# Cross attention's first half on one core: turning in two row tiles, key parts copied from SBUF to SBUF, and a new order of the work around them

## The reference

```
x = x + tanh(g_xattn) * xattn(ctx, ctx, layernorm(x), mask, wq, bq, wk, bk, wv, bv, wo, bo)
x = x + tanh(g_ffn)   * ffn(layernorm(x), Wq, Wk, Wv, Ws, Wd, Wo)

# xattn, for each batch
qh, kh, vh = heads(q @ wq + bq), heads(ctx @ wk + bk), heads(ctx @ wv + bv)
attn = softmax(qh @ kh.T / sqrt(16) + mask * -1e9)        # 16 x 112 x 375
out  = merge(attn @ vh) @ wo + bo
```

## Time and profile before

| what | value |
|---|---|
| median of 3 runs | 1317.49 us (1315.44 to 1321.64) |
| the profiled execution's own time | 1307.75 us |
| its span | 1306.0 us |
| mean granted TensorE clock | 0.986 of full speed |
| busy: PE, PEld, DVE, ACT, POOL | 1250.1, 1019.9, 860.6, 612.0, 549.9 us |
| first half, seen by its rows of PE | scores from 41 us to 660 us |

### The profile page before, as it was taken

How to read it: one execution, slowest core, us unless ns; L and a number is a source line. 1 busy time by engine, 2 the same in 40 slices (tenths; PEclk the granted TensorE clock), 3 DMA queues, 4 the chain that set the end, 5 groups by cost and what they waited for, 6 DMA issues and landing times. The chain is left out here.

```text
span 1306.0 us, 40359 instructions
## 1 busy us (share of the span) xinstructions
PE 1250.1 (96%) x15928; PEld 1019.9 (78%) x15928; DVE 860.6 (66%) x2455; ACT 612.0 (47%) x1353; POOL 549.9 (42%) x823
## 2 busy tenths in 40 slices
PE   5799999999999999999988999999999999999996
PEld 4577777777777777777767888888888888888885
DVE  2566766766776776766655676677667667766652
ACT  3455555556556556556423443443444344344431
POOL 3476676676676676666620221221222122122211
PEclk9899999999999999999989999999999999999997
DMA  8898897787787787786404665566566656656563
GB/s 231 186 192 189 192 202 166 165 185 162 164 185 159 159 185 155 159 189 145 104 18 110 145 138 156 139 141 143 138 143 138 157 136 141 142 139 148 138 156 91
DMA packets 262975, 200.21 MB, mean 153 GB/s; under 512 B 195906, under 2 KB 243844, under 8 KB 258692
## 3 DMA queue, kind: packets, MB, share of 16 engines
q1 hardware_dynamic: 262788, 197.64, 66.7%
HBM read 125.49 MB, written 72.11 MB: 151 GB/s over the span
## 5 line engine op out<-in xcount | busy, mean ns | idle before, releaser
L858 POOL TENSOR_SCALAR shifted<-raw,neg_max 112x375 f32<-112x375 f32 x512 | 304.5, 603 | 197.1 <-DVE neg_max L741 131.4
L741 DVE CUSTOM_DVE_ANT_0 raw<-bank_s,maskb 112x375 f32<-112x375 f32 x512 | 269.0, 544 | 119.4 <-issue 77.9
L653 ACT ACTIVATE probsT<-bank_t 128x448 f32<-128x448 f32 x384 | 181.1, 547 | 162.9 <-PE bank_t L446 162.9
L446 PE MATMUL bank_t<-ident,shifted 112*128 112x112 f32 x1536 | 170.7, 261 | 4.1 <-POOL shifted L858 4.1
L446 PEld LDWEIGHTS bank_t<-ident,shifted 112*128 112x128 f32 x1536 | 156.3, 141 | 22.7 <-POOL shifted L858 19.8
L437 PE MATMUL bank_s<-K_stack,Q_stack 128*112 128x375 bf16 x512 | 158.4, 337 | 12.8 <-DVE neg_max L741 8.2
L1381 DVE TENSOR_REDUCE max<-bank_s 112x4 f32<-112x448 f32 x128 | 78.7, 615 | 78.1 <-PE bank_s L1140 78.1
L1454 POOL TENSOR_TENSOR mix_bd<-pm_te,tok 128x448 f32<-128x448 f32 x32 | 30.4, 951 | 214.8 <-DMA pm_te<-pm_dram 214.8
L1092 PE MATMUL bank_ab<-xnT,wk2T 128*128 128x224 f32 x512 | 110.9, 360 | 0.6 <-ACT kT L1281 0.6
L1092 PE MATMUL bank_ab<-xnT,wq2T 128*128 128x224 f32 x512 | 110.8, 360 | 0.4 <-ACT qT L1273 0.4
L201 POOL TENSOR_SCALAR var_eps<-moments 112x1 f32<-112x1 f32 x32 | 7.1, 223 | 233.4 <-DVE moments L197 233.2
(11 more groups left out here) (141 smaller groups left out, 2227.4 us busy)
## 6 DMA issues: line engine op xcount, KB each, us to landing
K_stack<-k_dram SPq DMA_DIRECT2D x64, 562.5 KB, 7.3
k_dram<-k_parts SPq DMA_DIRECT2D x32, 562.5 KB, 5.0
att_dram<-att_q SPq DMA_DIRECT2D x32, 511.0 KB, 4.1
att_th<-att_dram SPq DMA_DIRECT2D x32, 511.0 KB, 4.3
v_dram<-mv SPq DMA_DIRECT2D x32, 455.0 KB, 6.1
v<-v_dram SPq DMA_DIRECT2D x32, 455.0 KB, 4.0
K_stack<-k_dram SPq DMA_DIRECT2D x32, 375.0 KB, 9.4
Q_stack<-q_dram SPq DMA_DIRECT2D x64, 168.0 KB, 9.3
```

Of the source, the lines that this page charges most:

```text
L446: last = nc.tensor.transpose(bank_t[0:KP, k, j * S:(j + 1) * S], shifted[:, g % 2, j, k * KP:(k + 1) * KP], c.ident[0:S, 0:S])
L653: act.activation(probsT[:, g % 2, k, :], bank_t[0:KP, k, 0:G * S], ACT.Exp).then_inc(exp_done, 1)
L741: dve.tensor_tensor_reduce(raw[:, g % 2, j, :], bank_s[h % 2][0:S, 0:S2], c.maskb[:, :], -1.0, -LEAST, ALU.add, ALU.min, neg_max[:, g % 2, ...
L858: pool.tensor_scalar(shifted[:, g % 2, j, 0:S2], raw[:, g % 2, j, :], -1.0, neg_max[:, g % 2, j:j + 1], ALU.mult, ALU.add).then_inc(shift_ ...
```

## The change

- **Turn.** Each transpose is cut into two: rows 0 to 63 and rows 64 to 111 of `shifted` (`HALVES`, as `switch` has it for its own turn). A unit u is one (chunk, head). The results lie in three banks as `PLACES` says, four stretches of 512, 480, 256 and 96 columns, and `exps` has one ACTIVATE for each. `turned` is raised once for a turn, not once for each bank, and PE waits for itself before unit 8 (`upper_done`).
- **Weigh.** `weigh(b, g)` stands ahead of `turn` of the next group wherever it can, and waits for all four exponentials.
- **Keys.** `k_dram` goes. SP copies each part from `k_parts` to its rows of `K_stack` with a transfer of its own for each half t: 128 partitions of 375 bf16 to 8 partitions of 16 x 375. That is 16 transfers for a batch, 6 ahead of the wait for the query parts and 10 behind the query stores. The wait for the scores of batch b-2 moves to the front.
- **Order.** On PE: S0 S1, weigh(b-1,2), transposes, turn(b-1,3), S2 S3 S4, keys 0, S5, weigh(b-1,3), turn(b,0), S6 S7, keys 1, heads_back, S8, weigh(b,0), turn(b,1), S9, heads_turn, S10, values 0 and 1, S11 S12, project, S13, turn_x, weigh(b,1), turn(b,2), S14 S15, values 2, queries. On DVE `split_queries` comes after the maxima of S0 to S3 instead of S0 and S1. On ACT `ctx_copy` comes ahead of `exps(b-1,3)`, and `copy_x` ahead of `exps(b,2)`.

```
+    DH = P // H
+    KEY_LOADS, QUERY_LOADS = 16 * EC * sum(n for _, n, _ in STACKED), 16 * len(STACKED)
+    UNITS, LOW = KC * G, z.S - 48
+    PLACES = ((0, 8, 0, 0, 0), (0, 10, 1, 1, 0), (8, 12, 0, 2, 0), (10, 12, 1, 2, 4 * LOW))
+    HALVES = ((0, LOW), (LOW, z.S))
...
             def exchange(b, p, i):
+                if not (isinstance(b, int) and b < 2):
+                    sp.wait_ge(scores_ready, H * (b - 1))
                 sp.wait_ge(k_split, b + 1)
-                sp.dma_start(by_partition(k_dram[bass.ds(b, 1)]), k_parts[:, p, :, :, :]).then_inc(k_stored[p], 16)
+                def stack_keys(blocks):
+                    for j, n, _ in blocks:
+                        for part in range(n):
+                            for t in range(EC):
+                                row = (j + part) * D + t * DH
+                                sp.dma_start(K_stack[row:row + DH, p, :, :],
+                                             k_parts[:, p, part, t, :]).then_inc(keys_stacked[p], 16)
+                stack_keys(STACKED[:1])
                 sp.wait_ge(q_split, b + 1)
...
-                if not (isinstance(b, int) and b < 2):
-                    sp.wait_ge(scores_ready, H * (b - 1))
-                sp.wait_ge(k_stored[p], 16 * i + 16)
-                for j, n, first in STACKED:
-                    sp.dma_start(K_stack[j * D:(j + n) * D, p, :, :].rearrange("d h k -> d (h k)"),
-                                 k_dram[bass.ds(b, 1), 0:n].rearrange("a q (d h) k -> (a q d) (h k)", h=H)).then_inc(stack_loaded[p], 16)
+                stack_keys(STACKED[1:])
                 sp.wait_ge(q_stored[p], 32 * i + 32)
...
...
             def turn(b, g, first):
                 pe.wait_ge(shift_done, H * b + G * g + G)
-                for k in range(KC):
-                    if not (first and g == 0):
-                        pe.wait_ge(exp_done, KC * (NG * b + g - 1) + k + 1)
-                    for j in range(G):
-                        last = nc.tensor.transpose(bank_t[0:KP, k, j * S:(j + 1) * S],
-                                                   shifted[:, g % 2, j, k * KP:(k + 1) * KP], c.ident[0:S, 0:S])
-                    last.then_inc(turned, 1)
+                if not (first and g == 0):
+                    pe.wait_ge(exp_done, len(PLACES) * (NG * b + g))
+                def one(half, u):
+                    lo, hi = HALVES[half]
+                    (bank, column), = [(bank, column + (u - first_u) * (hi - lo)) for first_u, end, h, bank, column in PLACES
+                                       if h == half and first_u <= u < end]
+                    k, j = u // G, u % G
+                    return nc.tensor.transpose(bank_t[0:KP, bank, column:column + hi - lo], shifted[lo:hi, g % 2, j, k * KP:(k + 1) * KP], c.ident[lo:hi, lo:hi])
+                for u in range(UNITS):
+                    if u == 8:
+                        pe.wait_ge(upper_done, NG * b + g + 1)
+                    one(0, u)
+                    last = one(1, (u + UNITS - 2) % UNITS)
+                    if u == 1:
+                        last.then_inc(upper_done, 1)
+                last.then_inc(turned, 1)
...
             def exps(b, g, first):
-                for k in range(KC):
-                    act.wait_ge(turned, KC * (NG * b + g) + k + 1)
-                    act.activation(probsT[:, g % 2, k, :], bank_t[0:KP, k, 0:G * S], ACT.Exp).then_inc(exp_done, 1)
+                act.wait_ge(turned, NG * b + g + 1)
+                for first_u, end, half, bank, column in PLACES:
+                    lo, hi = HALVES[half]
+                    act.activation(probsT[:, g % 2, first_u:end, lo:hi], bank_t[0:KP, bank, column:column + (end - first_u) * (hi - lo)].rearrange("p (u q) -> p u q", q=hi - lo),
+                                   ACT.Exp).then_inc(exp_done, 1)
```

More of the change, by code:

```diff
@@ L296, in cross @@
         k_rest_done, k_second, k_split = sem("k_rest_done"), sem("k_second"), sem("k_split")
-        k_stored = [sem(f"k_stored{i}") for i in range(2)]
-        stack_loaded = [sem(f"stack_loaded{i}") for i in range(2)]
+        keys_stacked = [sem(f"keys_stacked{i}") for i in range(2)]
+        queries_stacked = [sem(f"queries_stacked{i}") for i in range(2)]
         half_set = sem("half_set")
@@ L507, in body @@
                 if back:
-                    turn(b - 1, NG - 1, False)
-                S_(2)
+                    weigh(b - 1, 1 - p, NG - 2, False)
                 if ahead:
                     transposes(b + 2, i + 1, p)
-                S_(3)
                 if back:
-                    weigh(b - 1, 1 - p, NG - 1, False)
-                S_(4)
+                    turn(b - 1, NG - 1, False)
+                S_(2, 3, 4)
                 if ahead:
@@ L518, in body @@
                 S_(5)
+                if back:
+                    weigh(b - 1, 1 - p, NG - 1, False)
                 turn(b, 0, first)
@@ L530, in body @@
                 S_(8)
+                weigh(b, p, 0, first)
                 turn(b, 1, False)
@@ L540, in body @@
                     values(1 - p, 1).then_inc(va_ready, 1)
-                S_(11)
-                weigh(b, p, 1, False)
-                S_(12)
+                S_(11, 12)
                 if back:
@@ L552, in body @@
                     open_x(b + 2 - B)
+                weigh(b, p, 1, False)
+                turn(b, 2, False)
                 S_(14, 15)
@@ L600, in _ @@
             batches(pe, body)
+            weigh(B - 1, 1, NG - 2, False)
             turn(B - 1, NG - 1, False)
@@ L668, in body @@
                 second = isinstance(b, int) and b == 1
+                if ahead:
+                    ctx_copy(b + 2, p, False)
                 if not first:
@@ L671, in body @@
                 if ahead:
-                    ctx_copy(b + 2, p, False)
+                    key_copy(b + 2, p, i + 1, 0)
                 if not first:
                     heads_copy(b - 1, second)
-                if ahead:
-                    key_copy(b + 2, p, i + 1, 0)
                 exps(b, 0, first)
@@ L684, in body @@
                     key_second(b + 2, p)
+                if ahead:
+                    copy_x(b + 2)
                 exps(b, 2, False)
                 if ahead:
-                    copy_x(b + 2)
                     query_copy(b + 2, p, i + 1)
@@ L796, in body @@
                     o.moments_of(dve, c.X[0:S, b + 2 - B, :], b + 2 - B)
-                score_max(b, first, 0, 1)
+                score_max(b, first, *range(4))
                 if not first and not last:
                     split_queries(b + 1)
-                score_max(b, first, *range(2, 7))
+                score_max(b, first, *range(4, 7))
                 if ahead:
@@ L855, in shift @@
                     h = G * g + j
-                    free = [] if j or (first and g < 2) else [(turned, KC * (NG * b + g - 1))]
+                    free = [] if j or (first and g < 2) else [(turned, NG * b + g - 1)]
                     wait_all(pool, v_set, (scores_read, H * b + h + 1), *free)
```

19 lines of the change are left out of this document (8 added, 11 removed).

## The result

The changed kernel takes 1679.55 us (median of 4 runs, 1653.12 to 1687.08), the kernel before 1319.57 us beside it; the ratio is 1.2605 with a 95% interval of 1.2533 to 1.2677. It is formed from the undisturbed runs alone and so lies a little under the ratio of the medians. Forecast were 1308 us and a range up to 1480. The rival "keys late" had the sign, the place and, at its upper price of 1644 us, the size.

The account below looks back on a forecast made before the run. PE, busy 96%, was taken to bound the kernel at 19.41 us a batch; terms summed to 0.30 us saved a batch, 9 us over thirty, giving 1308 us, with an 8-in-10 range of 1288 to 1480 us.

Parts of the forecast that it names:

- keys late: Rival: S0 waits for `K_stack` or `Q_stack`; 1384 us at 1.13 us a transfer, 1644 at 1.76; chance 0.38.
- x: Time of one 96 KB key transfer from SBUF to 8 partitions; taken near the key store, SP's 0.47 us binding.
- the point where it turns: Time of one key transfer, 0.88 us, from which late stacks instead of PE's 19.1 us set the batch period.
- the signs that it named: Signs of being wrong: S0 waiting each batch, key transfers landing well over 2 us after issue, DMA share above 0.9.
- 10.3 + 10x: Time in us from a batch's S0 until the next stacks are ready, with ten key transfers ahead of the query loads.
- the late split: `split_queries` behind the maxima of S2 and S3: ends 5.65 us after S0 instead of 3.0; query stores issued until 6.6.
- SP's issue time: On SP's queue: 0.47 us for each key transfer, 7.5 us a batch for 16.
- The turn: On PE: 24 half transposes take 0.75 us instead of 1.15; four turns save 1.60 us a batch.
- S4 and S13: PE waits for score banks: S4 1.06 to 1.10 us behind S2, net cost 0.46; S13 1.47 behind S11, cost 0.29.
- PE's sum: PE's gain a batch: 1.60 - 0.45 - 0.46 - 0.29 - 0.10 = 0.30 us, 9 us over thirty batches.
- PE's own waits eat the gain: Rival: `upper_done` and dearer transpose pairs lose up to 0.46 us a batch, halfway 1320 us; chance 0.14.
- What was called hidden: On ACT: a fourth exponential, 0 to 0.43 us, and later exponentials, covered by weighting over 2.5 us behind its turn.

Follow-up runs that it names:

- the run with four fewer: Changed kernel without the last four of the ten key transfers behind the query stores from the third batch on: 1450.64 us, ratio 1.0996.

## Why the prediction was wrong, point by point

**The step that failed** is the choice of x, the time of one key transfer: "I take x near the key store, since pieces and source are its own, and consecutive transfers go to different partitions". The store's row told of the source and the pieces; what binds is the destination. Measured in the changed kernel: 1.75 us at the 55 GB/s of 431 to 436 us, 1.7 by the run with four fewer, against 0.47 taken and 0.88 as the point where it turns. That the form of the copy isn't to blame is shown by the run that changed the rows alone. The earlier trace rows had the warning, 215 GB/s into 48 or 32 partitions against 334 into 112, and the argument gave it less weight than the likeness of source. The prediction called this its weakest choice and gave late keys a chance of 0.38, but its range of 8 in 10 ended at x about 1.45. Of the signs that it named, S0 waited in every batch, but the DMA share wasn't above 0.9: it was 0.58 at the 55 GB/s.

The Trainium skill, page "SBUF — State Buffer", section "Door 1: The DMA port swizzle", put four neighbouring partitions on one port of 27 GB/s; its estimate was x = 1.76 us and 1640 us, measured were 1.7 to 1.75 and 1680. By that rule neighbouring rows reach 2 ports, rows 2 apart 4 and rows 4 apart 8, estimated 54, 109 and 218 GB/s; the traces have 55, 97 and 144, the last at SP's issue rate. The runs don't measure a port itself.

**What followed from x.** The rival's 10.3 + 10x with a late start of the last ten gave 30.3 us for the period at x = 1.76, measured 30.5. That is in part luck. The same sum gives 27.7 us with the early split (30.3 - 2.65), measured 23.4: x is no constant, it averages at most 1.46 us there. So the late split, which by that sum costs 2.65 us a batch or 80 us, is a large part of the loss where transfers are slow: with neighbouring rows an early one gives back 228 of the 360 us, with keys through DRAM 33. The sum also had the query stores issued from 5.65 us after S0; it was 427.67 - 420.30 = 7.4, with the clock at the lower level behind the wait.

**SP's issue time** was 0.65 us a transfer, not 0.47: the row used was for three loads of another shape. It does no harm in the changed kernel with rows 4 apart and three query loads. With four query loads and 12 key transfers behind the stores SP needs 2.6 us more, of the 3.3 by which the period is longer (22.9 against 19.6 us on average).

**The turn.** 411.10 - 410.21 = 0.89 us with one change of shape; the sum had 0.75 + 0.09 = 0.84. That is 0.2 us a batch of the 0.30 forecast.

**S4 and S13.** S4 starts 1.11 us behind S2 (forecast 1.06 to 1.10), S13 1.48 behind S11 (forecast 1.47).

**PE's sum.** Forecast 0.30 us a batch, 9 us. The kernel with keys through DRAM and early split, which is this sum without any wait for a stack, stands at 1.0022, with a period of 19.5 us where the sum had 19.1: nothing gained. The rival "PE's own waits eat the gain" is what this part came to; the dearer turn is half of it, the context's transposes waited 0.17 us for the query copies instead of 0.10, and the rest wasn't followed up.

**The late split** was costed only for the straight keys. With keys through DRAM it makes S0 wait 0.87 us and costs 2.4% (1.0266 against 1.0022). Nothing needed it late: with the split early again the new order runs at 19.5 us a batch.

**What was called hidden.** The fourth exponential is hidden. The later start of all four was said to be covered because each weighting comes well behind its turn; in the new order no such wait stands among those of the kernel with keys through DRAM and early split, and the turn alone in the old one shows the price without the cover and without the moved `copy_x`, 1.1%.

**Left open.** Why the batches of the kernel with the early split get 142 GB/s at one time and 55 at another, and with it why an early split gives back so much. That it has to do with which transfers are in flight together is shown by the two runs with another order; that they overlap across ways, or that the engines fall into step on one pair of ways, is only argued, and no run controls it.

## What to carry to other kernels

Price a DMA transfer by the partitions it writes and how they lie, not only by bytes, pieces and source; if the order of rows is free, as in a contraction, try rows 4 apart instead of neighbours, and count what the new order costs in other transfers. Look at how long SP is held in an issue: an issue that takes longer than its usual time says that the transfers in front of it drain slowly. When a block becomes cheaper, ask what its consumers' start depended on: a turn that was 0.26 us shorter but handed on its first bank 0.4 us later made the old order slower.

## What the runs showed of the hardware

- The same 16 transfers of 96 KB from 128 to 8 partitions: 1.7 to 1.75 us each (55 GB/s) to neighbouring rows in the changed kernel, 97 GB/s to rows 2 apart, 144 GB/s, which is about SP's 0.65 us of issue, to rows 4 apart. The kernel goes from 1679.55 to 1317.87 us by the step to rows 4 apart alone.
- The share of the 16 DMA engines stayed at about half while only such transfers ran, 0.58 at 55 GB/s and 0.50 at 144 GB/s.
- The time of such a transfer isn't fixed: at most 1.46 us on average in the kernel with the early split, with 142 GB/s at one time and 55 at another.
- Two orders of the same transfers differ by 4% to 5% in the kernel's time (1.1491 against 1.1067, 1.3202 against 1.2605).
- An issue on SP took 0.65 us for this shape, against 0.47 for the loads of the earlier trace rows.
